# Last rows' norms on VectorE, unread mask products in TensorE's waits at both ends, and the last three expert pairs with fused additions in another order

## What is computed

```
h   = LN(x)
l   = attention of 16 heads in windows of 128 rows on h @ proj_local
g   = attention of 16 heads in windows of 256 rows on h @ proj_global
f   = softmax(fusion_w)[0] * l + softmax(fusion_w)[1] * g
y   = LN(f) * gamma + beta
x1  = x + LN(y)
xt  = LN(x1)
e   = expert of each row: largest of 32 logits xt @ w_router; gate: its softmax
      (at most 320 rows per expert are taken, in order; the others get 0)
o   = gate * (silu(buf @ w_gate[e]) * (buf @ w_up[e])) @ w_down[e]
out = x1 + LN(xt + o)
```

## Time and profile before

| | us |
|---|---|
| median of 3 runs | 1514.15 |
| lowest and highest | 1512.36, 1518.76 |
| profiled execution | 1507.44 |
| its span, first to last instruction | 1505.4 |
| mean granted clock of TensorE in it | 0.979 |

### The profile page before, as it was taken

How to read it: one execution, slowest core, us unless ns; L and a number is a source line. 1 busy time by engine, 2 the same in 40 slices (tenths; PEclk the granted TensorE clock), 3 DMA queues, 4 the chain that set the end, 5 groups by cost and what they waited for, 6 DMA issues and landing times.

```text
span 1505.4 us, 37992 instructions
## 1 busy us (share of the span) xinstructions
PE 1415.0 (94%) x12904; PEld 1041.2 (69%) x12904; DVE 1207.4 (80%) x3495; ACT 898.0 (60%) x1919; POOL 731.2 (49%) x1133
## 2 busy tenths in 40 slices
PE   6789999999999999999999999999999847999994
PEld 4567777777777777777777777777776525777773
DVE  6577888888888888888888888888888753888885
ACT  3356777777777777767777767777776542222220
POOL 4114544554454555455555555444554340566665
PEclk9899999999999999999999999999999987999997
DMA  7997667666777767766767656566666303455640
GB/s 142 168 232 199 119 117 110 112 114 112 117 123 114 114 116 117 115 122 104 124 110 115 112 109 110 109 108 109 111 105 103 110 15 127 147 171 155 190 143 18
DMA packets 253409, 183.30 MB, mean 122 GB/s; under 512 B 29446, under 2 KB 251849, under 8 KB 253216
## 3 DMA queue, kind: packets, MB, share of 16 engines
q1 hardware_dynamic: 232976, 165.14, 57.8%
q10 hardware_dynamic: 13328, 12.00, 2.7%
q0 software_dynamic: 6912, 3.73, 1.1%
HBM read 55.78 MB, written 38.04 MB: 62 GB/s over the span
## 4 chain that ended last, share of the span: by engine, by line
PE 77%; SPq 5%; issue 4%; DVE 4%; DMA 4%; POOL 3%; ACT 2%; ACTq 0%; POOLq 0%; DVEq 0%
PE bank L1419 13%; PE bank L1578 9%; PE bank L1408 7%; PE bank L1537 6%; PE bank L1452 6%; PE bank L1383 5%; PE bank L1428 5%; PE bank L1449 4%; PE bank L1375 4%; PE bank L1398 3%; SPq L403 3%; PE bank L1378 2%; PE bank L1385 2%; PE bank L1591 2%; PE bank L1602 2%
## 5 line engine op out<-in xcount | busy, mean ns | idle before, releaser
L1019 DVE TENSOR_REDUCE mx<-bank 128x2 f32<-128x512 f32 (+1 forms) x768 | 511.6, 673 | 137.0 <-PE bank L1449 107.7
L758 ACT ACTIVATE pt<-bank 128x512 f32<-128x512 f32 x768 | 440.8, 592 | 143.1 <-PE bank L1385 123.1
L1419 PE MATMUL bank<-xnT,weff 128*128 128x256 f32 x1024 | 249.7, 387 | 3.1 <-DVE rest L1003 1.9
L548 POOL TENSOR_TENSOR parts<-rest,parts 128x512 bf16<-128x512 f32 x128 | 149.4, 1167 | 193.3 <-ACT parts L775 193.3
L1419 PEld LDWEIGHTS bank<-xnT,weff 128*128 128x128 f32 x1024 | 188.2, 192 | 28.9 <-issue 2.7
L1452 PE MATMUL bank<-stack 96*128 96x256 bf16 x1024 | 199.0, 276 | 8.6 <-DVE mx L1019 8.2
L1383 PE MATMUL bank<-stack 128*128 128x256 bf16 x1024 | 195.7, 272 | 3.4 <-ACT pt L758 2.9
L1452 PEld LDWEIGHTS bank<-stack 96*128 96x128 bf16 x1024 | 83.9, 98 | 96.6 <-DVE mx L1019 42.7
L769 ACT ACTIVATE parts<-bank,bqk 128x256 bf16<-128x256 f32 x256 | 106.8, 468 | 69.5 <-PE bank L1419 67.6
L1578 PE MATMUL bank<-eT,ew 128*128 128x320 f32 x512 | 145.4, 438 | 0.6 <-ACT eT L891 0.6
L1385 PE MATMUL bank<-tri,identb 128*128 128x226 bf16 x512 | 133.2, 260 | 0.0
(11 more groups left out here) (161 smaller groups left out, 2633.9 us busy)
## 6 DMA issues: line engine op xcount, KB each, us to landing
stack<-parts SPq DMA_DIRECT2D x384, 128.0 KB, 4.7
stack<-parts SPq DMA_DIRECT2D x768, 64.0 KB, 2.6
slots_scratch<-zeros ACTq DMA_DIRECT2D x16, 650.0 KB, 5.4
xr<-x SPq DMA_DIRECT2D x32, 256.0 KB
out<-obuf SPq DMA_DIRECT2D x32, 256.0 KB, 3.2
ew<-w_gate SPq DMA_DIRECT2D x32, 256.0 KB
ew<-w_up SPq DMA_DIRECT2D x32, 256.0 KB
ew<-w_down SPq DMA_DIRECT2D x32, 256.0 KB
```

Source lines behind the costliest of these rows:

```text
L758: act.activation(pt[:, u % PTR, :], S2[u % 2][:, :], ACT.Exp).then_inc(p_ready, 1)
L1019: dve.reduce_max(dst, src, AX.X).then_inc(s1_read, 1)
L1419: last = pe.matmul(bank[:, t * WIN:(t + 1) * WIN], weff[:, b, c, qk * D + t * P:qk * D + (t + 1) * P], xnT[:, par, c, :], start=(c == 0), ...
```

## The change

- inv_std: ve is made before nm, and a new semaphore nm_made tells when nm is there; the shift waits for it, and VectorE's moments wait for it instead of ve_made.
- Stage d from step 33 on (windows 30 and 31): ScalarE no longer does norm 1 and norm 2. VectorE computes (f - mean) * gamma, then * rstd + beta in scale_shift; in add_input it takes y - mean, then * rstd + x. Four operations each on 256 columns (two for each of the two row blocks q). They wait for the moments and for the power, not for the shift.
- Stage f in steps 34 and 35: VectorE does row_norm right behind the moments; ScalarE no longer.
- In step 35 ScalarE's norm_again moves from place 3 to place 18, and waits for xn2_ready in all steps.
- TensorE: keep_warm(n) issues n products of the mask operands, 512 bf16 columns each, into bank 2, where nobody reads them. 8 before the projection j = 3 of window 0, 12 before the wait for the first row scores; in step 35 6, then 10 behind y_ready, 4 behind z_ready, 12 behind x1_ready; 9 behind the logits of steps 34 and 35; before the experts 5, 14 behind slot_ready, 10 behind the last scatter's landing, 4 behind the landing of the first rows.
- Last three pairs (13, 14, 15): rows are centred (zb - mean) before the power is there, and one fused operation multiplies by rstd and adds erows. On VectorE pair 13 is finished before take_head(14), pair 14's second part before take_head(15), pair 15's first part before its second part's statistics. On GpSimd the powers stand between single row DMAs instead of between whole parts.

```diff
             def inv_std(n, w, par=0):
                 wait(pool, ln_var[n], w)
-                pool.tensor_tensor(nm[:, n, :], mv[:, n, :, 0], minus1[:, :], ALU.mult)
                 pool.tensor_tensor(ve[:, n, :], mv[:, n, :, 1], eps2[:, :], ALU.add).then_inc(ve_made[n], 1)
+                pool.tensor_tensor(nm[:, n, :], mv[:, n, :, 0], minus1[:, :], ALU.mult).then_inc(nm_made[n], 1)
                 wait(pool, ve_made[n], w)
...
+                wait(pool, nm_made[n], w)
                 wait(pool, rstd_made[n], w)
...
             def scale_shift(d):
-                wait(dve, n1_ready, d)
+                wait(dve, ln_var[1], d)
                 wait(dve, x1_ready, back(d))
-                dve.tensor_tensor(ybuf[:, :, :], fbuf[:, :, :], gamma_row[:, :].unsqueeze(1).to_broadcast([P, 2, D]), ALU.mult
-                                  ).then_inc(y_scaled, 1)
+                for q in range(2):
+                    last = dve.scalar_tensor_tensor(ybuf[:, q, :], fbuf[:, q, :], mv[:, 1, q, 0:1], gamma_row[:, :], ALU.subtract, ALU.mult)
+                last.then_inc(y_scaled, 1)
+                wait(dve, rstd_made[1], d)
                 wait(dve, y_scaled, d)
...
+                for q in range(2):
+                    last = dve.scalar_tensor_tensor(ybuf[:, q, :], ybuf[:, q, :], rstd[:, 1, q:q + 1], beta_row[:, :], ALU.mult, ALU.add)
+                last.then_inc(y_ready, 1)
             def add_input(d, at):
-                wait(dve, z_ready, d)
+                wait(dve, ln_var[2], d)
+                for q in range(2):
+                    last = dve.tensor_scalar(ybuf[:, q, :], ybuf[:, q, :], mv[:, 2, q, 0:1], None, ALU.subtract)
+                last.then_inc(z_ready, 1)
...
+                wait(dve, rstd_made[2], d)
+                wait(dve, z_ready, d)
+                for q in range(2):
+                    last = dve.scalar_tensor_tensor(x1[:, at, q, :], ybuf[:, q, :], rstd[:, 2, q:q + 1], xr[:, at, q, :], ALU.mult, ALU.add)
+                last.then_inc(x1_ready, 1)
+            def row_norm(f, par):
+                wait(dve, ln_var[3], f)
+                wait(dve, rstd_made[3], f)
+                wait(dve, x2T_full, back(f))
+                wait(dve, o_norm, back(f))
+                for q in range(2):
+                    last = dve.tensor_scalar(xn2[:, q, :], x1[:, par, q, :], mv[:, 3, q, 0:1], xrow[:, par, q, RSTD:RSTD + 1], ALU.subtract, ALU.mult)
+                last.then_inc(xn2_ready, 1)
...
                     if f and k == at["moments_x1"]:
                         moments(3, f)
+                        if num(s) > LATE:
+                            row_norm(f, par)
...
             def late_rows(p, k):
...
+                dve.wait_ge(ne_ready, part_count(p, k))
                 for n in range(lo, hi):
-                    dve.tensor_scalar(zb[:, r, n, :], zb[:, r, n, :], mv_e[:, p % 2, n, 0:1], rs_e[:, p % 2, n:n + 1],
-                                      ALU.subtract, ALU.mult).then_inc(ne_ready, 1)
-                for n in range(lo, hi):
-                    dve.wait_ge(ne_ready, PAIRS - 3 + (p - PAIRS + 3) * NCH + n + 1)
-                    dve.tensor_tensor(zb[:, r, n, :], zb[:, r, n, :], erows[:, r, n, 0:D], ALU.add).then_inc(oe_ready, 1)
+                    dve.scalar_tensor_tensor(zb[:, r, n, :], zb[:, r, n, :], rs_e[:, p % 2, n:n + 1], erows[:, r, n, 0:D],
+                                             ALU.mult, ALU.add).then_inc(oe_ready, 1)
...
+            third, second, last = PAIRS - 3, PAIRS - 2, PAIRS - 1
+            hidden(2 * second)
+            take_rest(third)
+            row_stats(third, 0, 0, NCH)
+            hidden(2 * second + 1)
+            centre(third, 0)
+            late_rows(third, 0)
+            take_head(second)
+            row_stats(second, 0, 0, HALF)
+            centre(second, 0)
+            hidden(2 * last)
+            late_rows(second, 0)
+            take_rest(second)
+            row_stats(second, 1, HALF, NCH)
+            centre(second, 1)
+            hidden(2 * last + 1)
+            late_rows(second, 1)
+            take_head(last)
+            row_stats(last, 0, 0, HALF)
+            centre(last, 0)
             take_rest(last)
+            late_rows(last, 0)
             row_stats(last, 1, HALF, NCH)
-            late_rows(last, 0)
+            centre(last, 1)
             late_rows(last, 1)
...
+            def keep_warm(n):
+
+                for _ in range(n):
+                    pe.matmul(banks[2][:, :], identb[:, :], tri[:, :].unsqueeze(1).to_broadcast([P, 4, P]), start=True, stop=True)
+
```

GpSimd's order of the last three pairs (with late_rows(p, lo, hi) for single chunks):

```diff
+            rstd_part(third, 0)
+            late_rows(third, 0, HALF + 1)
+            rstd_part(second, 0)
+            late_rows(third, HALF + 1, NCH)
+            late_rows(second, 0, 1)
+            rstd_part(second, 1)
+            late_rows(second, 1, NCH - 1)
+            rstd_part(last, 0)
+            late_rows(second, NCH - 1, NCH)
+            late_rows(last, 0, HALF)
+            rstd_part(last, 1)
+            late_rows(last, HALF, NCH)
```

More of the change, by code:

```diff
@@ L205, in attention_moe_program @@
         ve_made = [sem(f"ve_made{n}") for n in range(5)]
+        nm_made = [sem(f"nm_made{n}") for n in range(4)]
         rstd_sq_made = sem("rstd_sq_made")
@@ L679, in add_pair, with late_rows @@
                     rows_out(p, n)
-            def late_rows(p, k):
-                for n in range(*parts_of(p)[k]):
+            def late_rows(p, lo, hi):
+                for n in range(lo, hi):
                     pool.wait_ge(oe_ready, rows_done(p, n))
@@ L805, in norm_again @@
                 wait(act, ln_rstd[4], w)
+                wait(act, xn2_ready, w)
                 for q in range(2):
@@ L837, in step @@
                         exps(k, c)
-                    if f and k == at["xn2"]:
+                    if f and num(s) <= LATE and k == at["xn2"]:
                         wait(act, x2T_full, back(f))
@@ L937, in moments @@
                 wait(dve, stats_made[n], w)
-                wait(dve, ve_made[n], back(w))
+                wait(dve, nm_made[n], back(w))
                 for q in range(2):
@@ L1293, in scale_rows, with centre @@
                 last.then_inc(ne_ready, 1)
+            def centre(p, k):
+                r = p % RING
+                lo, hi = parts_of(p)[k]
+                dve.wait_ge(me_made, part_count(p, k))
+                for n in range(lo, hi):
+                    last = dve.tensor_scalar(zb[:, r, n, :], zb[:, r, n, :], mv_e[:, p % 2, n, 0:1], None, ALU.subtract)
+                last.then_inc(ne_ready, 1)
             def late_rows(p, k):
@@ L1322, in _ @@
                     scale_rows(p - 1)
-                if p + 2 < PAIRS:
-                    norms(p + 2)
-            last = PAIRS - 1
+                norms(p + 2)
+            third, second, last = PAIRS - 3, PAIRS - 2, PAIRS - 1
+            hidden(2 * second)
[6 more added lines that the diff above has]
+            row_stats(second, 0, 0, HALF)
@@ L1413, in project @@
             def project(j, a, s, par):
+                if num(a) == 0 and j == 3:
+                    keep_warm(8)
                 wait_read(pe, PJ_USES, f"p{j}", s, 2)
@@ L1477, in step @@
                     out_bias()
+                if num(s) == NW + 3:
+                    keep_warm(6)
+                    wait(pe, y_ready, f)
+                    keep_warm(10)
+                    wait(pe, z_ready, f)
+                    keep_warm(4)
+                    wait(pe, x1_ready, f)
+                    keep_warm(12)
                 for k in range(UNITS):
```

41 lines of the change are left out of this document (17 added, 24 removed).

## The result

| | before | after |
|---|---|---|
| median of 5 runs, us | 1514.15 | 1506.51 |
| lowest and highest | 1511.07, 1518.76 | 1501.01, 1506.90 |
| profiled execution | 1507.44 | 1501.01 |
| its span | 1505.4 | 1499.0 |
| its mean granted clock | 0.979 | 0.991 |

The ratio is 0.9946, 95% interval 0.9926 to 0.9966: about 8 us faster. The forecast was 1502.5 with a range of 1496 to 1509. The ratios of this document are those of the record; they are not exactly the quotients of the two medians beside them.

The account below looks back on a forecast made before the run. The bound was taken as half clock in the head, small-operation chains in the last windows, and GpSimd's queue at the end. Norms 3.4, products 3.7, end 2.5 make 9.6; with the head's 2.0, 11.6: 1514.15 to 1502.5 us, range 1496 to 1509.

Parts of the forecast that it names:

- norm 1: Last windows: four VectorE operations replace ScalarE's norm and two 512-column passes, ending at 1227.3 instead of 1228.3, gain 1.0 us.
- norm 2: Last windows: a subtraction and a fused add on VectorE, 1.45 us, replace shift, hand-over, ScalarE and a pass; gain 0.6.
- The head's 2.0: Unread products between start and first exponential keep the clock full: 2.0 us in the timed runs, between 0 and 4.
- Norms, 3.4 us forecast: Steps 33 to 35: norms moved from ScalarE to VectorE, with earlier powers, save 3.4 us, ends 1.5 and 5.
- norm 3: Last windows, row norm on VectorE: 1.4 us become 0.75, with the earlier power a gain of 0.8.
- The order of ve and nm, the new wait: GpSimd's power no longer waits behind a fresh result: 0.15 us per norm on the chain; the moments' new wait costs nothing.
- Products, 3.7 us forecast: Steps 34, 35 and first expert: unread products keep TensorE's clock full, saving 3.7 us, ends 0 and 4.
- Rival B: The clock falls anyway between window steps and experts, or covers leak: 3.7 + 2.0 go, 1508 us. Chance 18%.
- End, 2.5 us forecast: Last pairs: earlier rows let GpSimd's queue of row DMAs start earlier, ending 1496.1 against 1498.6: 2.5 us, ends 1 and 3.5.
- D: Unread products run at half clock, 0.43 us each: 8.9 us lost against 5.9 kept, 1517 us. Chance 6%.
- E: SBUF port: fused adds hold up GpSimd's last DMAs and powers, 4 us, the end's gain gone: 1505 to 1507. Chance 6%.
- C: The head pays in full in the timed runs (4 or more), VectorE's norms at their upper end: 1498 us. Chance 17%.

Follow-up runs that it names:

- the second set: The changed kernel run once more with no edit, against the kernel before: median 1502.04 us (8 runs), ratio 0.9915.
- the 22: Runs of the unchanged kernel before, beside the repeat of the changed kernel: median 1514.45 us, 1507.45 to 1518.3.

## Why the forecast held, point by point

The direction holds, and the size within its range: forecast 11.6 us on the median, measured 7.6 and 12.4 in two sets of runs. The mechanism holds for norms, products and end: 9.6 us forecast, and by intervals 2.7 to 2.9, 2.6 to 3.3 and 2.3, in sum 7.6 to 8.5. The head's 2.0 are not confirmed, and some 4 of the 12.4 us no interval shows. That the second set came so near to 11.6 is therefore in part luck; the first set is near to what the intervals give.

- *Norms, 3.4 us forecast.* 2.9 in the trace without the fall: 0.9 up to f of window 31 (1.0 forecast), 2.0 behind it (2.4 forecast: norm 1 gives 0.7, norm 2 0.5, norm 3 0.7, against 1.0, 0.6 and 0.8). The missing 0.4 is for the most part one mis-sized term, in norm 1 above all, where two pairs stand. I took 0.37 us for a fused operation on 256 columns, from the rows of plain ones; it takes 0.44:

```profile
1227.88 0.88 DVE L1143 SCALAR_TENSOR_TENSOR ybuf<-ybuf,rstd,beta_row 128x256 f32<-128x256 f32 x2
...
1231.00 0.61 DVE L1150 TENSOR_SCALAR ybuf<-ybuf,mv 128x256 f32<-128x256 f32 x2
```

 Three pairs of them stand on this path: 3 x 0.14 = 0.42 us. The price of 0.42 for the operation reading PSUM, the upper end that I gave, was nearer than the value that I chose. The subtraction with one scalar is cheaper, 0.3 us, which gives 0.07 back.
- *The order of ve and nm, the new wait.* The power starts 0.29 us after the first of the two operations instead of 0.42: 0.13 against 0.15 forecast. Nobody waits for nm_made. No run has that edit alone.
- *Products, 3.7 us forecast.* 3.3 between x2T of window 31 and the second expert in the pair of first profiles (0.67 + 0.50 + 2.16), 2.6 to 2.7 against the kernel without products. The first expert's products take 4.55 us, not the 4.31 that I took from a later expert. Of the 3.3 some belong to norm_again's move: with the products alone the first of the three intervals stayed at 6.00. That interval has two gates, TensorE's clock and ScalarE's place for norm_again, and opening one shows nothing. I had put the whole 0.75 down to the clock.
- *"With TensorE so filled from 1222 on I take it that the clock never falls."* From f of window 31 to the experts it held in every trace with the products (granted 1.00 from 1222 to 1258 in the kernel after) but the one with norm_again early, where a wait of 1.85 us (0.62 in the kernel after) came before a fall of 3.4 us at 1248.1. The stretch just ahead, which nobody filled, had a fall in five of the eight traces of kernels with the new norms and without products there, 1.6 to 1.7 us each. I had read from one trace that the clock was full there. Rival B was right about this place, and wrong about the experts.
- *Head, 2.0 us forecast.* Not confirmed: 2.1 us between the medians with and without, inside the noise, and nothing in the traces that stands out of their spread. I had two reasons. The first, that the timed runs of before are worse than its profile, is right: the granted clock of the 22 is mostly 0.976 to 0.978 against 0.979 in the profile, and the shortest of them took 1507.45, as long as the profiled one. The second, that the clock falls already behind the waits of 29 and 34 us, is right too, in four of the five traces without the products, and the products put that fall off. What it lacked is that the clock falls again in the next waits, so that little is left of it by window 3. The longer traces differ in waits for SyncE's transfers up to window 5, which the products do not touch. The Trainium skill (TensorE: Matmul & The Clock Gate, The HAM clock gate, What's actually happening) says that the same kernel shows its transitions elsewhere from run to run; the two traces of the same kernel agree with it, with falls at 47.4, 61.0 and 1218.1 us in one and at 43.2, 70.5, 91.0, 145.6, 585.9 and 1231.0 in the other.
- *End, 2.5 us forecast, 2.3 measured,* but not by GpSimd's queue alone. I had GpSimd issuing without a gap but for the last fused addition. Its timeline after has gaps:

```profile
1484.08 0.97 POOL L670 DMA_INDIRECT out<-zb,idx_e  x1 [0.74 <-DVE zb L1339]
1485.35 0.97 POOL L670 DMA_INDIRECT out<-zb,idx_e  x1 [0.30 <-issue]
1486.34 0.90 POOL L665 TENSOR_TENSOR rs_e<-ve_e,mhalf 128x3 f32<-128x3 f32 x1
1488.56 1.04 POOL L670 DMA_INDIRECT out<-zb,idx_e  x1 [1.33 <-DVE zb L1339]
...
1491.17 0.97 POOL L670 DMA_INDIRECT out<-zb,idx_e  x1 [0.30 <-issue]
```

 Data and queue decide in turn: VectorE has the last part's variances at 1485.22 (L1312), but GpSimd is inside a row DMA until 1486.32, so the last power starts 1.1 us late, and the last three rows behind it. The last issue ends at 1492.14, 10.8 us after TensorE's end at 1481.33; the data bound of the forecast was 9.4, and the 1.1 us of that queue is nearly all of the difference. The forecast's own bound was 10.6, and that it is so near hides two errors that nearly cancel: from the first issue of pair 14's last rows (1479.06) to the end it is 13.1 us against 12.8 forecast, with powers 0.4 shorter than I had and the gaps between the issues 0.6 longer, the wait of 0.74 for VectorE among them. A power ahead of the second of these row DMAs would take some of it; it was not tried.
- *Rivals.* D (products at half clock, slower) did not happen: eight take 1.89 and twelve 2.75 us in the head, all at full clock. E (the port): such a stall is in the trace of before, where of the five norms of the earlier trace rows (L1238, 4.29 us) one takes 2.99 us, as long as GpSimd's addition beside it (2.93), and the rest about 0.4 each. At the end of the kernel after little of it is left: of the fifteen row DMAs of the last three pairs thirteen take 0.97 to 1.07; the two longer ones, 1.30 at 1466.86 and 1.25 at 1471.74, stand beside fused additions, but 10 us ahead of TensorE's end and off the path. The powers of pair 15 take 0.72 and 0.90, less than the 0.9 and 1.16 of the forecast. The Trainium skill's lock (SBUF — State Buffer, SBUF: two separate sides) is said to hold between a VectorE operation with two SBUF inputs and a GpSimd operation that reads SBUF, a condition that the forecast left out; those two DMAs, 0.3 us over the rest, are all among the row DMAs that could be such a lock here, and the five fused additions of pair 13 beside one of them took 2.07 us, 0.41 each. C asked for 4 us from the head and the upper end of the norms; neither came. The loss of the head's gain had no rival of its own with its cause, and should have had: the clock falls again in the waits behind it.

## What to carry to other kernels

Split such a forecast by intervals between the same instructions, and ask for each interval which waits end late in it without the change: here they were good to 0.4 us, but for the one where the clock fell, while single profiles of one program differed by 12. Unread products pay where the wait that they fill is longer than they are and the work behind is on the path (2.7 us here); one beyond the cover costs almost its full 0.22 us, and where more waits follow, as in the head, they put the fall of the clock off and pay nothing that can be seen. When a norm moves to another engine, look at what still stands in the old one's queue: at its old place norm_again would have cost 1.3 us. And when the timed gain is larger than all intervals together, as here by up to 4 us, say so and leave the rest open.

## What the runs showed of the hardware

- scalar_tensor_tensor on 128 x 256 f32 from SBUF with a scalar per row takes 0.41 to 0.44 us each (a pair 0.88, five 2.07); tensor_scalar with one scalar 0.28 to 0.32 (a pair 0.61, five 1.39, three 0.96).
- The clock fell to half where TensorE had no wait over 1.3 us since 1203 us, only short ones (0.78, 0.92 and 1.22 the longest, ahead of the fall at 1218.1), and not in all executions.
- One execution of an unchanged program differs from another by 10 us before its window 5, in two steps (88 or 92 us, then 72 to 78 us). The second goes with TensorE's wait for one transfer (0.7 to 4.2 us); the cause of the first is open.
- One of five norms on VectorE took 2.99 us beside an addition of 2.93 us on GpSimd, the rest about 0.4 each (trace of before, 1457.6).
